# A graph network step with a one-hot scatter on TensorE: 16-bit places loaded in half turns, a later input transfer, and one one-hot in eight on GpSimd

## The reference

```
sums = segment_sum(edge_attr, src, num_segments=6250)
counts = segment_sum(ones, src, num_segments=6250)
agg = sums / maximum(counts, 1)[:, None]
h = relu(concatenate([x, agg, u[batch]], axis=1) @ W1 + b1)      # batch is all zeros
y = layernorm(x + (h @ W2 + b2))                                 # 6250 x 256
```

## Time and profile before

| | |
|---|---|
| median of 3 runs | 801.16 us (800.42 to 801.40) |
| profiled execution, span from first to last instruction | 799.5 us |
| mean granted TensorE clock | 0.994 |
| PE busy in the span | 745.1 us, 93% |
| DVE busy | 716.8 us, 90% |
| ACT busy | 501.7 us, 63% |
| POOL busy | 417.1 us, 52% |

### The profile page before, as it was taken

How to read it: one execution, slowest core, us unless ns; L and a number is a source line. 1 busy time by engine, 2 the same in 40 slices (tenths; PEclk the granted TensorE clock), 3 DMA queues, 4 the chain that set the end, 5 groups by cost and what they waited for, 6 DMA issues and landing times.

```text
span 799.5 us, 31269 instructions
## 1 busy us (share of the span) xinstructions
PE 745.1 (93%) x11398; PEld 711.5 (89%) x11399; DVE 716.8 (90%) x2382; ACT 501.7 (63%) x998; POOL 417.1 (52%) x410
## 2 busy tenths in 40 slices
PE   8889999999999999999999888989898986899995
PEld 4689999999999999999999888989898986899995
DVE  8999999999999999999896388989898988799995
ACT  1366676666667767667667545555555552688886
POOL 3087777777677787877776400000000002788983
PEclk9999999999999999999999999999999999999999
DMA  6366556666665666656674678999999990012122
GB/s 215 131 210 204 201 202 211 213 215 219 202 219 195 212 220 211 225 205 214 203 210 167 239 227 260 281 282 282 285 283 285 281 277 10 27 52 64 53 66 64
DMA packets 75268, 156.38 MB, mean 196 GB/s; under 512 B 11084, under 2 KB 51277, under 8 KB 75097
## 3 DMA queue, kind: packets, MB, share of 16 engines
q1 hardware_dynamic: 58328, 102.33, 42.5%
q0 software_dynamic: 16896, 53.54, 17.9%
HBM read 95.47 MB, written 60.37 MB: 195 GB/s over the span
## 4 chain that ended last, share of the span: by engine, by line
PE 60%; DVE 30%; issue 5%; ACT 2%; POOL 1%; DMA 1%; DVEq 0%; ACTq 0%; SPq 0%; POOLq 0%
PE ps L858 33%; DVE onehot L1236 18%; PE ps L785 11%; PE ps L936 5%; PE ps L990 3%; DVE pre L1275 2%; DVE perm L1146 2%; DVE stats L1301 1%; DVE weights_z L1296 1%; PE ps L776 1%; PE ps L792 1%; POOL h_low L628 1%; PE ps L811 1%; PE ps L843 1%; PE ps L841 1%
## 5 line engine op out<-in xcount | busy, mean ns | idle before, releaser
L600 POOL DMA_INDIRECT sorted_rows<-payload,idx x264 | 304.8, 1155 | 131.8 <-issue 51.9
L858 PE MATMUL ps<-attr_buf,perm 128*128 128x198 bf16 x3168 | 302.6, 252 | 1.1 <-ACT attr_buf L642 0.8
L858 PEld LDWEIGHTS ps<-attr_buf,perm 128*128 128x128 bf16 x3168 | 288.6, 96 | 6.1 <-ACT attr_buf L642 1.2
L649 ACT CAST payload<-ps 128x792 bf16<-128x792 f32 x264 | 217.9, 825 | 76.7 <-PE ps L858 62.2
L1146 DVE TENSOR_SCALAR perm<-place_of,pos 128x512 bf16<-128x512 int16 x792 | 241.1, 362 | 3.4 <-PE ps L858 2.7
L1236 DVE TENSOR_SCALAR onehot<-node_of,sup 128x256 bf16<-128x256 int16 x903 | 192.4, 284 | 41.9 <-PE ps L936 22.3
L936 PE MATMUL ps<-sup,onehot 128*128 128x64 bf16 (+1 forms) x6192 | 196.1, 193 | 24.7 <-DVE onehot L1236 21.0
L936 PEld LDWEIGHTS ps<-sup,onehot 128*128 128x128 bf16 x6192 | 193.5, 98 | 27.3 <-issue 27.3
L619 POOL TENSOR_TENSOR xs<-xs,b_all 125x256 f32<-125x256 f32 x50 | 37.6, 775 | 209.4 <-DMA xs<-in_x 209.4
L713 ACT ACTIVATE apart<-node_of,sup 128x256 bf16<-128x256 int16 x129 | 65.6, 508 | 94.3 <-PE ps L936 90.2
L785 PE MATMUL ps<-xt,w1x 128*128 128x125 f32 x800 | 99.9, 278 | 5.9 <-DVE pos L1067 3.3
(11 more groups left out here) (150 smaller groups left out, 603.7 us busy)
## 6 DMA issues: line engine op xcount, KB each, us to landing
sup<-sorted_rows SPq DMA_DIRECT2D x129, 396.0 KB, 4.0
attr_buf<-in_edge_attr SPq DMA_DIRECT2D x43, 576.0 KB
out<-weights_z SPq DMA_DIRECT2D x25, 224.0 KB
xs<-in_x SPq DMA_DIRECT2D x12, 448.0 KB
x_stage<-in_x SPq DMA_DIRECT2D x47, 112.0 KB
sorted_rows<-payload,idx POOLq DMA_INDIRECT x264
pre<-jump_d SPq DMA_DIRECT2D x1, 1560.0 KB, 10.4
pre<-first_d SPq DMA_DIRECT2D x1, 780.0 KB, 7.2
```

The costliest lines, as they stand in the source:

```text
L600: pool.indirect_dma_start(out=sorted_rows, out_offset=bass.IndirectOffsetOnAxis(ap=idx[:, n:n + 1], axis=0), in_=payload[s][:, :], in_offs ...
L649: nc.scalar.copy(payload[s][:, :].rearrange("p (r w) -> p r w", w=PART), slots_p[s % PSUM_BUFS]).then_inc(s_pay, 1)
L858: last = nc.tensor.matmul(slot_p[s % PSUM_BUFS][r].rearrange("p (h f) -> p h f", f=PLANE), places, parts(a, t * CB + s), start=(t == 0 and ...
```

## The change

1. `where`, `where_d` and `where_row` hold 16-bit instead of 32-bit integers, and `where_row` is now the first tensor in SBUF.
2. PE loads its places eight registers at a time. `find_tables(1, ..)` stands ahead of super 4 of a turn and loads those of supers 8 to 15; `find_tables(0, ..)` stands ahead of super 12 and loads those of supers 0 to 7 of the next turn. The load of 16 at a turn's start is gone. Turn 0 is written out ahead of the loop, on PE and on DVE.
3. From turn 1 on slot 3 of odd supers is made by POOL (121 one-hots, written out without a loop), which waits for `s_sup` and `s_added` as DVE does; PE waits for it with `s_hot_p`.
4. SP transfers `xs` behind its last super, in 5 pieces of 10 columns with a semaphore each. POOL's additions of `b2` stand behind its last one-hot, and it waits for a piece where it first needs it.

```diff
-X_TURN = 3
-X_COLS = 4
+AHEAD = PAIR_BUFS // 2
+X_COLS = 10
...
-    where_d = nc.dram_tensor("where_d", [2, SUPER_COLS * P], I32, kind="Internal").ap()
+    where_d = nc.dram_tensor("where_d", [2, SUPER_COLS * P], U16, kind="Internal").ap()
...
+        where_row = sb("where_row", [1, 2 * SUPER_COLS * P], U16)
         ident = sb("ident", [P, P])
...
-            for m in range(1, X_TURN):
+            with sp.Fori(1, SUP_TURNS) as m:
                 super_turn(m)
+            super_turn(SUP_TURNS, SUPER_PAIRS - SUP_TURNS * PAIR_BUFS)
+
             sp.wait_ge(s_pre, COLS + 1)
-            with sp.Fori(X_TURN, X_TURN + X_PIECES) as m:
-                super_turn(m)
+            for k in range(X_PIECES):
                 for lo, hi in ((0, XPART), (XPART, NP)):
...
+                    sp.dma_start(xs[lo:hi, k * X_PIECE:(k + 1) * X_PIECE], x_v[lo:hi, k * X_PIECE:(k + 1) * X_PIECE]
+                                 ).then_inc(s_xs[k], 16)
...
+            def super_turn(m, count=BODY):                       # GpSimd
+                for k in range(1, count, 2):
+                    pool.wait_ge(s_sup[k // 2], m * 16 + 16)
+                    pool.wait_ge(s_added, m * BODY + (k + 1 + SUP_FREE - HOT_BUFS))
+                    nc.gpsimd.tensor_scalar(onehot[k % HOT_BUFS][:, ACT_SLOT, :], node_of[:, :],
+                                            place_in[k][:, ACT_SLOT, :], None, ALU.is_equal).then_inc(s_hot_p, 1)
+
+            for m in range(1, SUP_TURNS):
+                super_turn(m)
+            super_turn(SUP_TURNS, 2 * SUPER_PAIRS - SUP_TURNS * BODY)
             pool.wait_ge(s_b2, 16)
-            pool.wait_ge(s_xs, 2 * 16 * (X_PIECES + 1))
...
+                if g % (X_COLS // 2) == 0:
+                    pool.wait_ge(s_xs[g // (X_COLS // 2)], 2 * 16)
...
-            def super_turn(m, count=BODY):                       # TensorE
-                pe.load(table_regs[0:count], where_row[0:1, bass.ds(m * BODY, count)])
+            def find_tables(half, at):
+                pe.load(table_regs[half * PAIR_BUFS:(half + 1) * PAIR_BUFS], where_row[0:1, bass.ds(at, PAIR_BUFS)])
+
+            def super_turn(m, count=BODY, first=False):
                 for k in range(count):
+                    if k == PAIR_BUFS - AHEAD:
+                        find_tables(1, m * BODY + PAIR_BUFS)
+                    if k == BODY - AHEAD:
+                        find_tables(0, m * BODY + BODY)
...
                     if k % 2 == 0:
                         pe.wait_ge(s_hot_a, m * PAIR_BUFS + (k // 2 + 1))
+                    elif not first:
+                        pe.wait_ge(s_hot_p, m * PAIR_BUFS + (k // 2 + 1 - PAIR_BUFS))
...
-                    for r in range(SLOTS - 1 + k % 2):           # VectorE
+                    for r in range(SLOTS - 1 + (k % 2 if first else 0)):
```

More of the change, by code:

```diff
@@ L97 @@
 SUP_TURNS = SUPER_PAIRS // PAIR_BUFS
+AHEAD = PAIR_BUFS // 2
+assert 2 * SUPER_PAIRS - SUP_TURNS * BODY <= PAIR_BUFS
+assert (ZERO_SUPER + 1) * P < 65536
 ACT_SLOT = SLOTS - 1
@@ L114 @@
 Z_BUFS = 3
-assert X_TURN + X_PIECES + 1 == SUP_TURNS
+assert X_PIECES * X_COLS == COLS and X_COLS % 2 == 0 and X_COLS // 2 >= B2_AHEAD
 STEPS = COLS // 2
@@ L151, in build @@
         eps_col = sb("eps_col", [P, 1])
-        where_row = sb("where_row", [1, 2 * SUPER_COLS * P], I32)
         node_of = sb("node_of", [P, 2 * P], I16)
@@ L214, in build @@
         beyond = edge_sb("beyond", [P, SUPER_COLS])
-        where = edge_sb("where", [P, 2, SUPER_COLS], I32)
+        where = edge_sb("where", [P, 2, SUPER_COLS], U16)
         chosen = edge_sb("chosen", [P, SOON * E1])
@@ L363, in build @@
         s_hot_a = sem("s_hot_a")
+        s_hot_p = sem("s_hot_p")
         s_apart = sem("s_apart")
@@ L366, in build @@
         s_table = sem("s_table")
-        s_xs = sem("s_xs")
+        s_xs = [sem(f"s_xs{k}") for k in range(X_PIECES)]
         s_xb = sem("s_xb")
@@ L940, in super_turn @@
                     last.then_inc(s_added, 1)
-            with pe.Fori(0, SUP_TURNS) as m:
+            find_tables(0, 0)
+            super_turn(0, first=True)
+            with pe.Fori(1, SUP_TURNS) as m:
                 super_turn(m)
@@ L1227, in _, with super_turn @@
             chunk(CHUNKS - 1, (CHUNKS - 1) % TURN, None)
-            def super_turn(m, count=BODY):
+            def super_turn(m, count=BODY, first=False):
                 for k in range(count):
@@ L1238, in super_turn @@
                     last.then_inc(s_hot_d, 1)
-            with dve.Fori(0, SUP_TURNS) as m:
+            super_turn(0, first=True)
+            with dve.Fori(1, SUP_TURNS) as m:
                 super_turn(m)
```

## The result

The changed kernel takes 840.02 us (median of 4 runs, 838.68 to 840.5) where the kernel before took 800.79 in the same set of runs: a ratio of 1.048, 95% interval 1.0464 to 1.0499. It is 39 us slower, where the prediction was 796.3 with a range to 804. The profiled execution spans 838.7 us at a mean granted TensorE clock of 0.993 (before 0.994), so the clock is not the cause of the 39 us.

What follows compares the result with a forecast made beforehand. PE bounds the supers, losing 1.46 us at each turn's end. Out: 22.5 + 1.8 = 24.3 us; in: 15.6 (loads) + 3.8 (branch) = 19.4; 4.9 less gives 794.6 in the profile, 796.3 as median, range 781 to 804.

Steps and rivals of the forecast that it cites:

- What bounds the kernel, the load at the turn's end: Supers: PE loses 1.46 us at each of 15 turn ends; removing that load, with the last end, gains 22.5 us.
- the branch: PE's loop branch at the turn's end stays, 14 times at 0.27 us each, 3.8 us.
- Whether a load stops the sequencer: PE's register loads in the supers: not shown by the rows, taken as blocking; each stops PE for 0.52 us.
- the lead: PE's sequencer runs some 0.5 us ahead of the array; 0.53 us is subtracted from each stop.
- The first rival: PE's loads do not stop the sequencer and are hidden whole: 15.6 us more gained, 780.7 us; chance 0.16.
- What a load costs: PE's load of eight 16-bit places: 0.55 us, priced per 32 bytes; 30 loads cost 15.6 us.
- The rival with the right mechanism, a cost by the register: PE's loads cost 0.79 us each, 7.2 us more in all, 803.5 us, slower; chance 0.10 for over 0.75.
- The formula around it: PE's stop per load: 0.10 address, the load, 0.10 to next instruction, 0.30 to first matmul, less 0.53.
- GpSimd's one-hot worth nothing, a hold of 0.25 us on DVE: Odd supers: takes one 0.196 us DVE operation per pair, gains nothing; holds DVE for 0.25 us.
- The third rival: GpSimd's one-hot makes DVE the bound from a hold of 0.46 us: 799 to 815 us; chance 0.14.
- The input behind the supers, 1.79 us: Moving xs and POOL's additions behind the supers removes two PE stops in the last turn, gaining 1.79 us.
- The floor of the Trainium skill: Register loads take at least about 600 ns; by it 30 loads cost 1.5 us more, 797.8 us.

Runs made afterwards that it cites:

- the probe: Kernel before plus 15 PE loads of 1 to 16 registers ahead of the supers; four aligned 32-bit registers took 335 ns, eight 16-bit ones 1917 ns.
- a3_no_pool: Changed kernel with all of slot 3 of odd supers on DVE again, without POOL's one-hots and PE's wait for them: 841.81 us, ratio 1.051.
- a2_before_u16: Kernel before with only the places (where, where_d, where_row) in 16 bits, still one load of 16 registers per turn: 861.04 us.

## Why the prediction was wrong

*What bounds the kernel, the load at the turn's end*: right. The 15 stops of 1.46 us went. In the kernel with 32-bit places, where nothing else grew, the turn is 13.12 us, which is the prediction's own number. That it fits to the last digit is luck: the loads lasted 0.59 instead of 0.55 (0.08 a turn) and the branch cost 0.17 instead of 0.27. The total fits by luck too: in that trace turn 1 took 15.2 us, 2.1 more than forecast, and turn 0 0.7 less.

*Whether a load stops the sequencer*: right, and now shown. In the changed kernel an instruction that needs nothing of the load starts only behind it, and the stop is as long as the load less the lead. The first rival, hidden loads and 780.7 us, is out.

*What a load costs*: **the step that failed**. "8 bytes at 0.556, 32 bytes at 0.537 and 64 bytes at 1.10 look like a price per 32 bytes rather than per register; eight 16-bit places are 16 bytes, so I take 0.55." It is 1.93. The rows were of 32-bit registers only, and the step turned them into bytes to read off a load of 16-bit ones; the probe shows that bytes set the price only in aligned pieces of four 32-bit registers. The rival with the right mechanism, a cost by the register, was bounded at 0.79 by the line through two registers (one by one) and sixteen (four pieces), which are paid by different prices. The same row of two registers held a bound that was not drawn: 0.556 / 2 = 0.28 a register, 2.2 us for eight, some 847 us for the kernel. Where the trace had no load of that type, the range had to reach there; it ended at 804.

*The formula around it* (0.10 + load + 0.10 + 0.30 - 0.53): right. With 1.93 it gives 1.90 us lost per load, measured 1.87 (1.9 from start to start, less a step of 0.03). With 0.59 it gives 0.56, measured 0.51 to 0.56.

*The sum with the measured load*: 30 stops cost 1.87 each (1.9 from start to start, less a step of 0.03) instead of 0.52, 40.5 us more; 794.6 + 40.5 = 835.1 in the profile. The loop's branch costs 0.17 instead of 0.27 in 14 turns, 1.4 less. The rest to 838.7 is some 5 us. Turn 0 takes 17.3 us as before, though the 1.46 at its end are gone, 1.4 us more than in the sum, where its two loads are taken at nothing. The clock has a part in that. Two pieces of turn 0 of the changed kernel:

```profile
456.00:458.00 2.00, 2.00 (x41) 2.00 (x39) 1.57 (x9) 1.42 (x4) 0.00 (x0) 0.50 1.05 384
458.00:460.00 2.00, 2.00 (x41) 2.00 (x39) 1.51 (x7) 0.71 (x2) 0.00 (x0) 0.50 1.06 388
```

Its first 96 matmuls last 5.35 us at 0.50, 2.2 more than at full pace; before, the low clock there was over by 456 to 458 us (0.95) and cost 1.5. In `a3_no_pool`, which has the same loads and was granted 1.00 there, turn 0 took 15.4 us, but its turn 1 took 18.0, with the low clock in it. How much the loads themselves cost in the first turns is not settled by that. Matmuls come 0.2 ns later each, some 1.4 us, for which I have no cause (`a3_no_pool` has it too, so it is not GpSimd's one-hots). The first super starts 2.7 us later, 0.8 of it the first load, which lasts 2.12 instead of 1.30. The other 1.9 us ahead of that load are open: it starts at 451.2 us in `a2_before_u16` and in `a3_no_pool`, which has the changed kernel's loads, and at 452.7 in the changed kernel, so neither the type nor the loads account for it. Behind the supers 0.6 us is gained.

*GpSimd's one-hot worth nothing, a hold of 0.25 us on DVE*: right, for a reason partly wrong. The two one-hots of DVE in the rows below start at 566.14 and 566.56, the first beside one of POOL's (all of POOL's last 1.02 us, page above):

```profile
L1257 DVE TENSOR_SCALAR onehot<-node_of,sup x1: 503/503/503, 566.1 to 566.1; 128x256 bf16<-128x256 int16 x1
L1257 DVE TENSOR_SCALAR onehot<-node_of,sup x1: 276/276/276, 566.6 to 566.6; 128x256 bf16<-128x256 int16 x1
```

The one beside POOL is 0.50 us and the next comes 0.42 us after it instead of 0.196, a hold of 0.23; in the whole stage it is the same beside 119 of the 121. The one-hot itself was forecast at 0.41 us from the casts and lasts 1.02, 2.5 times as long, and it doesn't matter: POOL had 1.6 us for each. The third rival, decided from a hold of 0.46, didn't come. The Trainium skill ("SBUF — State Buffer", Who interferes with whom) says that of GpSimd and a DVE operation in a two-port mode the one that issues first has the shared ports for its whole instruction. The trace differs here: DVE is held for 0.23 us of GpSimd's 1.02.

*The input behind the supers, 1.79 us*: right in the trace of the kernel with that alone, whose last turn has no stop in it; too small to settle in its times.

*The floor of the Trainium skill* ("DMA: Bandwidth & Descriptors", Latency and other measured facts, about 600 ns): the trace differs. One 16-bit register takes 0.303 us, four aligned 32-bit ones 0.335; eight 16-bit ones take three times the floor.

## What to carry to other kernels

Before a register load is moved to where it is paid more often, price it by its own type and alignment. If the trace has no load of that type, take the dearest reading of the nearest rows as the bound, per register as well as per byte, and let a term that counts thirty times set the range. When two engines are each said to wait for the other, look at the sequencer's own rows between them; and put an instruction that blocks it in the middle of a run of matmuls, not beside the register work at its seams.

## What the runs showed of the hardware

- A register load on PE costs 0.34 us for the first aligned piece of four 32-bit registers and about 0.25 for each further one (335, 602, 845, 1104 ns for 4, 8, 12, 16), and 0.23 us for each register otherwise (16 bits, or 32 bits from the second element on: 1948 ns for eight). Two or three 32-bit registers (553, 771 ns) cost more than four.
- SP pays for the type too: its eight places take 1.66 us in the changed kernel, where they took 0.694. DVE waited 16.8 us in all for SP's transfers, before 17.4, so it cost nothing there.

```profile
L506 SPq TENSOR_LOAD <-where_row x17: 273/1660/2232, 436.5 to 694.8; - x17
```

- After 3.9 us without a matmul PE was granted 0.50 (1.2 GHz) for 2 to 3 us of its next work, which made each such stop 1.2 us dearer; after the 1.7 us of the changed kernel's loop it was not. `a3_no_pool` shows it once after a stop of 1.85 us that came soon behind one of 0.40: 192 matmuls lasted 7.58 us instead of 6.1, granted 0.51 in part.

```profile
471.59 1.22 PE L943 MATMUL ps<-sup,onehot 128*128 128x65 bf16 x34 [0.40 <-issue]
474.66 7.58 PE L943 MATMUL ps<-sup,onehot 128*128 128x64 bf16 x192 [1.85 <-DVE onehot L1245]
...
476.00:478.00 2.00, 2.00 (x44) 2.00 (x41) 1.41 (x8) 0.78 (x3) 0.00 (x0) 0.51 0.22 25
```

- A comparison of 128x256 int16 to bf16 lasts 1.02 us on GpSimd and 0.28 on DVE, and holds DVE for 0.23.
